# Inner values of a mixture-of-experts layer made by feature, with the weights as the stationary operand

## The reference

```python
w, sel = jax.lax.top_k(probs, K)            # K = 8 of E = 64 experts
w = w / jnp.sum(w, axis=-1, keepdims=True)
...
valid = pos < CAP                            # CAP = 64 rows for each expert
...
h = jax.nn.silu(jnp.einsum('ech,ehi->eci', inp, wg)) * jnp.einsum('ech,ehi->eci', inp, wu)
out = jnp.einsum('eci,eih->ech', h, wd)      # h = 256, i = I = 96
...
g = out_pad[eid, slot] * (w.reshape(-1) * valid.astype(w.dtype))[:, None]
y = jnp.zeros((T, Hd), x.dtype).at[tok].add(g)
```

## Time and profile before

| | us |
|---|---|
| median of 3 runs | 418.92 |
| lowest, highest | 418.79, 421.54 |
| the profiled execution, whole | 416.79 |
| its span, first to last instruction | 415.0 |

### The profile page before, as it was taken

How to read it: one execution, slowest core, us unless ns; L and a number is a source line. 1 busy time by engine, 2 the same in 40 slices (tenths; PEclk the granted TensorE clock), 3 DMA queues, 4 the chain that set the end, 5 groups by cost and what they waited for, 6 DMA issues and landing times.

```text
span 415.0 us, 5198 instructions
## 1 busy us (share of the span) xinstructions
PE 265.8 (64%) x1680; PEld 166.5 (40%) x1680; DVE 230.4 (56%) x519; ACT 130.3 (31%) x230; POOL 163.7 (39%) x165
## 2 busy tenths in 40 slices
PE   4748766599896958877659693620089999960000
PEld 4635535366574626664345432310045555420000
DVE  0747553568777649668462845150057777540393
ACT  5300382007930039511096204010024444230022
POOL 2220022300227742247700287127606478477073
PEclk9897899679997799988969969565579999995555
DMA  7699999970192320962200299200069998966791
GB/s 260 168 133 345 358 386 195 260 206 2 38 134 92 133 86 2 118 111 105 73 2 0 76 343 318 70 25 9 1 194 300 318 192 175 309 99 69 265 383 66
DMA packets 47261, 66.61 MB, mean 161 GB/s; under 512 B 5979, under 2 KB 33241, under 8 KB 47234
## 3 DMA queue, kind: packets, MB, share of 16 engines
q1 hardware_dynamic: 39120, 56.52, 49.3%
q0 software_dynamic: 7680, 9.47, 11.5%
q10 hardware_dynamic: 434, 0.27, 0.2%
HBM read 36.45 MB, written 28.75 MB: 157 GB/s over the span
## 4 chain that ended last, share of the span: by engine, by line
PE 28%; issue 19%; DVE 15%; DMA 12%; ACT 10%; another core or an unknown queue 6%; POOL 5%; SPq 3%; POOLq 0%; DVEq 0%; ACTq 0%
PE M L1052 11%; PE O L1052 6%; DMA acc_d<-xp_t,idx_out 5%; PE SA L1052 3%; DMA early<-early 3%; ACT probs L530 3%; SPq L343 3%; POOL xin_d L451 3%; DVE nmax L763 2%; PE SB L1052 2%; PE O L1398 2%; DVE early L1012 1%; DMA early<-acc_d 1%; ACT xp L553 1%
## 5 line engine op out<-in xcount | busy, mean ns | idle before, releaser
L451 POOL DMA_INDIRECT xin_d<-row,idx_slot x64 | 63.2, 988 | 24.7 <-issue 18.8
L489 POOL DMA_INDIRECT acc_d<-xp_t,idx_out x32 | 49.4, 1544 | 34.5 <-DVE idx_out L988 15.1
L471 POOL TENSOR_TENSOR early<-early 128x1024 f32<-128x1024 f32 x4 | 8.5, 2133 | 86.3 <-ACT early L540 86.3
L1052 PE MATMUL SA<-early 96*128 96x256 bf16 (+1 forms) x128 | 24.4, 325 | 20.1 <-ACT early L594 9.5
L1052 PE MATMUL SB<-early 96*128 96x256 bf16 (+1 forms) x128 | 23.9, 319 | 6.4 <-DVE nmax L763 5.0
L763 DVE TENSOR_REDUCE nmax<-SA 128x4 f32<-128x1024 f32 x16 | 19.5, 1218 | 13.2 <-PE SA L1052 13.2
L1398 PE MATMUL O<-con,probs 128*128 128x128 f32 x40 | 9.2, 319 | 26.2 <-DMA probs<-xin_d 26.2
L1052 PEld LDWEIGHTS SA<-early 96*128 96x128 bf16 (+1 forms) x128 | 12.3, 110 | 31.5 <-issue 12.4
L763 DVE TENSOR_REDUCE nmax<-SB 128x4 f32<-128x1024 f32 x16 | 19.5, 1220 | 9.6 <-PE SB L1052 5.3
L659 ACT ACTIVATE xp<-M 128x96 f32<-128x96 f32 x32 | 8.0, 251 | 51.8 <-PE M L1052 47.8
L1052 PE MATMUL O<-xf,early 128*128 128x256 f32 x64 | 18.6, 445 | 6.4 <-DMA early<-weights 5.2
(11 more groups left out here) (201 smaller groups left out, 644.3 us busy)
## 6 DMA issues: line engine op xcount, KB each, us to landing
gu_sb<-wgu SPq DMA_DIRECT2D x20, 384.0 KB
acc_d<-zeros SPq DMA_DIRECT2D x3, 2176.0 KB, 19.0
early<-early SPq DMA_DIRECT2D x48, 128.0 KB, 5.4
early<-acc_d SPq DMA_DIRECT2D x24, 256.0 KB, 7.5
xin_d<-zeros SPq DMA_DIRECT2D x1, 5136.0 KB, 23.2
early<-wgu SPq DMA_DIRECT2D x12, 384.0 KB
wd_sb<-wd SPq DMA_DIRECT2D x20, 192.0 KB
probs<-xin_d SPq DMA_DIRECT2D x20, 160.5 KB
```

Source lines behind the costliest of these rows:

```text
L451: nc.gpsimd.indirect_dma_start(xin_d, bass.IndirectOffsetOnAxis(ap=idx_slot[:, t, k:k + 1], axis=0), row[:, t, :], None, bounds_check=SLOT ...
L471: nc.gpsimd.tensor_tensor(rest[:], qk[:], parts[:, :, 0], ALU.subtract).then_inc(S["rest_r"], 1)
L489: nc.gpsimd.indirect_dma_start(acc_d[p % CHAINS], bass.IndirectOffsetOnAxis(ap=idx_out[:, p:p + 1], axis=0), yw[:, p % YRING, :], None, bo ...
L1052: return nc.tensor.matmul(o, l, r, start=start, stop=stop)
```

## The change

The gate and up product swaps its operands: the weights are stationary, [128 features x 96], and the gathered rows move, 64 columns. For gate and for up, for each expert and for each half of the features, there is one matmul, eight a pair in place of four. The results stand by feature: `M[0:96]` with gate in columns 0 to 127 and up in 128 to 255, the 128 rows of both experts side by side. So `hid` is made in the form in which the down product takes it. The turn on PE and the copy on ACT go, with their semaphores. The row weight can't be a scalar of each partition any more while features stand on the partitions; it now scales the eviction of the down product, which has rows on the partitions, once for each expert. The factor 0.5 moves into `hid`. PE works on three pairs at once in place of four. The load of rows `p + 10` waits for the evictions of pair `p`, which now read its gathered rows last.

```diff
@@ -379,7 +378,7 @@
             follows = {(p - LATE - RING if p - LATE - RING < RING else p - RING): p for p in range(RING + LATE, PAIRS)}
             for p in range(PAIRS):
                 if p + GRING < PAIRS:
-                    sp.wait_ge(S["hid"], 2 * (p + 1))
+                    sp.wait_ge(S["yw"], 2 * (p + 1))
                     sp.wait_ge(S["idx_out"], p + 1)
                     load_rows(p + GRING)
                 if p in follows:
...
-                pool.wait_ge(S["yw"], p + 1)
+                pool.wait_ge(S["yw"], 2 * (p + 1))
                 if p >= CHAINS:
 
                     pool.wait_ge(S["scat"][p % CHAINS], 16 * (p // CHAINS))
@@ -650,26 +649,24 @@
             pipelined(act, iteration)
 
 
-            for i in range(PAIRS + 3):
+            for i in range(PAIRS + 2):
                 if 1 <= i <= PAIRS:
                     p = i - 1
                     act.wait_ge(S["gu_mm"], p + 1)
                     if p >= 2:
                         act.wait_ge(S["hgate"], p - 1)
-                    nc.scalar.activation(htanh[:, p % 2, :], M[:, p % 2, 0:INNER], ACT.Tanh, scale=0.5).then_inc(S["htanh"], 1)
-                if 2 <= i <= PAIRS + 1:
+                    nc.scalar.activation(htanh[:, p % 2, :], M[0:INNER, p % 2, 0:P], ACT.Tanh, scale=0.5).then_inc(S["htanh"], 1)
+                if i >= 2:
                     p = i - 2
-                    act.wait_ge(S["hid_mm"], p + 1)
-                    if p >= 2:
-                        act.wait_ge(S["wd_mm"], p - 1)
-                    nc.scalar.activation(hid_f[:, p % 2, :], slot[p % 2][0:INNER, 512:512 + P], ACT.Copy).then_inc(S["hid_ev"], 1)
-                if i >= 3:
-                    p = i - 3
                     act.wait_ge(S["wd_mm"], p + 1)
                     if p >= YRING:
                         act.wait_ge(S["scat"][(p - YRING) % CHAINS], 16 * ((p - YRING) // CHAINS + 1))
-
-                    nc.scalar.activation(yw[:, p % YRING, :], slot[p % 2][:, 0:D], ACT.Copy, scale=0.5).then_inc(S["yw"], 1)
+                    for e in range(2):
+
+                        h = slice(e * CAP, (e + 1) * CAP)
+                        c = D + 2 * p + e
+                        nc.scalar.activation(yw[h, p % YRING, :], slot[p % 2][h, 0:D], ACT.Copy, scale=gath(p)[h, c:c + 1]
+                                             ).then_inc(S["yw"], 1)
 
             for t in range(TILES):
                 act.wait_ge(S["fshift"], t + 1)
@@ -994,17 +991,13 @@
                 if i >= 1:
                     p = i - 1
                     dve.wait_ge(S["htanh"], p + 1)
-                    nc.vector.scalar_tensor_tensor(hgate[:, p % 2, :], htanh[:, p % 2, :], 1.0, M[:, p % 2, 0:INNER],
+                    nc.vector.scalar_tensor_tensor(hgate[:, p % 2, :], htanh[:, p % 2, :], 1.0, M[0:INNER, p % 2, 0:P],
                                                    ALU.add, ALU.mult).then_inc(S["hgate"], 1)
                     dve.wait_ge(S["hgate"], p + 1)
                     if p >= 2:
-                        dve.wait_ge(S["hid_mm"], p - 1)
-                    for e in range(2):
-
-                        h = slice(e * CAP, (e + 1) * CAP)
-                        c = D + 2 * p + e
-                        nc.vector.scalar_tensor_tensor(hid[h, p % 2, :], hgate[h, p % 2, :], gath(p)[h, c:c + 1],
-                                                       M[h, p % 2, INNER:2 * INNER], ALU.mult, ALU.mult).then_inc(S["hid"], 1)
+                        dve.wait_ge(S["wd_mm"], p - 1)
+                    nc.vector.scalar_tensor_tensor(hid[:, p % 2, :], hgate[:, p % 2, :], 0.5, M[0:INNER, p % 2, P:2 * P],
+                                                   ALU.mult, ALU.mult).then_inc(S["hid"], 1)
 
 
             def halves_added(t):
...
@@ -1403,27 +1396,21 @@
                     pe.wait_ge(S["xin"], p + 1)
                     pe.wait_ge(*loaded(p))
                     if p >= 2:
-                        pe.wait_ge(S["hid"], 2 * (p - 1))
+                        pe.wait_ge(S["hid"], p - 1)
+                    for u in range(2):
+                        for e in range(2):
+                            for c in range(NC):
+                                m = mm(M[0:INNER, p % 2, u * P + e * CAP:u * P + (e + 1) * CAP], place(p)[0][:, e, c, u, :],
+                                       xin[:, p % 2, c, e * CAP:(e + 1) * CAP], c == 0, c == NC - 1)
+                    m.then_inc(S["gu_mm"], 1)
+                if i >= 2:
+                    p = i - 2
+                    pe.wait_ge(S["hid"], p + 1)
+                    if p >= 2:
+                        pe.wait_ge(S["yw"], 2 * (p - 1))
                     for e in range(2):
                         h = slice(e * CAP, (e + 1) * CAP)
-                        for c in range(NC):
-                            m = mm(M[h, p % 2, 0:2 * INNER], xin[:, p % 2, c, h],
-                                   place(p)[0][:, e, c].rearrange("p u i -> p (u i)"), c == 0, c == NC - 1)
-                    m.then_inc(S["gu_mm"], 1)
-                if 2 <= i <= PAIRS + 1:
-                    p = i - 2
-                    pe.wait_ge(S["hid"], 2 * (p + 1))
-                    if p >= 2:
-                        pe.wait_ge(S["hid_ev"], p - 1)
-                    nc.tensor.transpose(slot[p % 2][0:INNER, 512:512 + P], hid[:, p % 2, :], ident).then_inc(S["hid_mm"], 1)
-                if i >= 3:
-                    p = i - 3
-                    pe.wait_ge(S["hid_ev"], p + 1)
-                    if p >= 2:
-                        pe.wait_ge(S["yw"], p - 1)
-                    for e in range(2):
-                        h = slice(e * CAP, (e + 1) * CAP)
-                        m = mm(slot[p % 2][h, 0:D], hid_f[:, p % 2, h], place(p)[1][:, e])
+                        m = mm(slot[p % 2][h, 0:D], hid[:, p % 2, h], place(p)[1][:, e])
                     m.then_inc(S["wd_mm"], 1)
 
 
```

More of the change, by code:

```diff
@@ L181, in build @@
         flat = xp[:].rearrange("p t h m -> p (t h m)")
-        htanh, hgate, hid = (flat[:, i * 2 * INNER:(i + 1) * 2 * INNER].rearrange("p (g s) -> p g s", g=2)
-                             for i in range(3))
-        gath_b = flat[:, 6 * INNER:6 * INNER + (GRING - in_probs) * ROW].rearrange("p (g r) -> p g r", g=GRING - in_probs)
+        htanh, hgate = (flat[0:INNER, i * 2 * P:(i + 1) * 2 * P].rearrange("p (g s) -> p g s", g=2) for i in range(2))
+        gath_b = flat[:, 4 * P:4 * P + (GRING - in_probs) * ROW].rearrange("p (g r) -> p g r", g=GRING - in_probs)
         def gath(p):
@@ L189, in gath @@
             return gath_a[:, r] if r < in_probs else gath_b[:, r - in_probs]
-        hid_f = mix_a[:].rearrange("p t h d -> p (t h d)")[0:INNER, 0:2 * P].rearrange("p (g s) -> p g s", g=2)
+        hid = mix_a[:].rearrange("p t h d -> p (t h d)")[0:INNER, 0:2 * P].rearrange("p (g s) -> p g s", g=2)
         flat = xp_t[:].rearrange("p t j q -> p (t j q)")
@@ L264, in build @@
                   "idx_out", "gt_mm", "xin", "gu_mm", "htanh",
-                  "hgate", "hid", "hid_mm", "hid_ev", "wd_mm", "yw", "fadd", "fpair", "fstat", "fmv", "fvar", "fshift",
+                  "hgate", "hid", "wd_mm", "yw", "fadd", "fpair", "fstat", "fmv", "fvar", "fshift",
                   "frstd", "fout", "stored", "passed"):
```

## The result

The changed kernel takes 477.12 us (median of 4 runs, 476.67 to 477.41) where the kernel before takes 420.23 in the same set: the ratio is 1.140, 95% interval 1.135 to 1.145. I had predicted 422.2. The profiled execution has a span of 475.6 us, 60.6 over that of before.

What follows compares the result with a forecast made beforehand. Scatters with their landings (2.27 us a step) bound the kernel before; PE at 2.43 would bound the new one. Last scatter 3.3 us later: span 418.3, run 420.1, plus 2.1 to the median: 422.2 us, range 420 to 424.5.

Steps and rivals of the forecast that it cites:

- The start: Start of the experts' stage: clock 1.00 after 306.8 us, first down product at 308.4 where it was 308.69.
- the cycle: PE's time for a pair in the experts' stage: 0.58 + 0.37 + 1.48 = 2.43 us against 2.00.
- Rival D: Experts' stage: clock falls as the array streams less; at 0.50 a pair takes over 4 us, some 60 us; chance 0.04.
- rival B: Gate and up product: records cost moving passes alone, 1.98 us a pair, not slower, 418.5 us; chance 0.13.
- The price of a record: Gate and up product: loading 96 stationary columns sets the pace, 0.084 us a record, bounds 0.054 and 0.111.
- C: Gate and up product: loads cost as for 128 columns, 2.84 us a pair, 435 us in all; chance 0.07.
- PE as the new bound: Experts' stage: PE's 2.43 us a pair exceeds the scatters' 2.27, so PE sets the pace.
- +0.8%: Whole kernel: predicted time of 422.2 us as a change from the median of 418.92.
- The two halves of the eviction: ACT after the down product: two scaled halves take 0.85 us, bounds 0.78 and 0.94, where one took 0.39.
- DVE and the handovers: Between product and down product: DVE instructions near 0.29 us each, four handovers of some 0.05; DVE hidden before and after.
- The moved wait: SP's load of rows p+10 waits for the scaled eviction of p, about one PE cycle later: free.
- rival E: Experts' stage: scatter stalls add to slower PE, two or three of 1 to 2 us, 424 to 427; chance 0.15.

Runs made afterwards that it cites:

- the run in blocks: Changed kernel, but pairs 0 to 7 and 16 to 23 stream 96 gathered rows a matmul, the other pairs 64: 425.16 us, ratio 1.009.
- 96 rows: Changed kernel, but each of the product's eight matmuls streams 96 gathered rows in place of 64, the extra results unread: 403.36 us, ratio 1.007.
- four wide pairs: Changed kernel, but pairs 0 to 3 alone stream 96 gathered rows in each product matmul; pairs 4 to 31 stream 64: 406.50 us, ratio 1.012.
- the matmuls ahead: Changed kernel plus 28 unread matmuls of 128x128 by 512 columns on PE before the experts' stage; all pairs stream 64: 399.95 us, ratio 0.995.
- 128 rows: Changed kernel, but each of the product's eight matmuls streams all 128 gathered rows in place of 64, half unread: 414.19 us beside 400.27.
- the run with the scaled eviction alone: Kernel before, product and turn kept; only row weights move to the eviction in two halves, and row loads wait for it: 405.28 us, ratio 1.014.
- the run that goes wide there: Changed kernel, but pairs 16 to 31 stream 96 gathered rows in each product matmul, pairs 0 to 15 stream 64: 430.23 us beside 402.30.

## Why the prediction was wrong

**The step that failed is "The start".** It took from the earlier trace rows that the clock is 1.00 from 306.8 us on, and carried that over. But in the earlier trace rows the clock rose while the old product ran, which streams 192 columns a matmul; I used the rise as if it belonged to the place in the program and not to what PE does there. In the changed kernel it never comes, and each of the three pieces of the cycle takes 1.7 to 1.9 times as long: 2.51, 1.05 and 0.62, against 1.33, 0.58 and 0.37 with the clock up (the run in blocks). Of the 4.18 - 2.00 = 2.18 us that a pair gained, 1.90 are the clock and 0.28 the new form.

**Rival D had it, with 60 us, and I gave it 0.04.** What I held against it was a row with the clock at 1.00 over eight records of 64 moving columns. That stretch lies behind work that had brought the clock up. It shows that such records keep a full clock, which the experiments bear out (28 narrow pairs at 1.00), and nothing on whether they raise it from half. D was also put as a clock that falls during the stage; measured, it doesn't fall, it fails to rise. The page of the Trainium skill that I cited for rival B (TensorE: Matmul & The Clock Gate) also says, in its Part 1, The HAM clock gate, that PE's clock is low after idle time and rises when PE is kept busy. The trace agrees on the first half and not on the second: 32 pairs with PE busy for every microsecond of the windows, and 0.50 to the end.

**The price of a record was right, the cycle somewhat too long.** I had 0.084; the narrow product at full clock is 1.33/16 = 0.083, and 0.164 at half. But the cycle is 2.28, not 2.43: I added the whole tail of 0.22 to the product, most of which lies in the piece of the chain that follows and was counted there already (0.58 and 0.37 are measured from start to start). The order of the terms was right: it is the load of 96 columns, not the 64 streamed, that sets the pace, so rival B's 1.98 is out, and so is C's 2.84. The section of the Trainium skill that I cited for B (TensorE: Matmul & The Clock Gate, Back-to-back issue gap) gives its rule by moving columns for a single matmul, and says itself that in a stream of loads and matmuls both set the spacing. The trace agrees with the latter: 0.083 where the moving columns alone would give 0.054.

**PE as the new bound: right in kind.** With the clock up, a step of 2.28 is level with the scatters' 2.27, and the time is within 1.2% of the kernel before (1.007 with 96 rows, 1.012 with four wide pairs, 0.995 with the matmuls ahead). With 128 rows PE's 2.70 sets the end. The changed kernel's own instructions on a clock that is up from the start are the run with 28 matmuls ahead, at 0.995 (interval 0.991 to 0.999), so my +0.8% would have been somewhat high there too. A part of that may be the first products at full clock, which the forecast had at half; no run separates it.

**The other terms.** The two halves of the eviction take 0.47 and 0.48 with the handover between, 0.98 together, where I had 0.85 and called the upper bound 0.94. DVE and the handovers were hidden, as said. The moved wait I had called free; the run with the scaled eviction alone says that this part costs 1.4% (0.5 to 2.2) where PE is quick, by a way that isn't separated. The stalls of the scatters (rival E) played no part: at 4.18 a pair POOL waits for ACT at nearly every scatter.

## What to carry to other kernels

Where a stage begins after PE has been idle, its clock is part of what a change can break: look in the rows at which instructions the clock rose, and ask whether the new ones would raise it too. A row at 1.00 shows that work of its kind can keep the clock, not that it can raise it. A change that loads weights more often and streams less should be tried with a few dense matmuls ahead of the stage before its form is given up: here that turned +14% into -0.5%, each beside the kernel before of its own set; the changed kernel itself ran only in the first.

## What the runs showed of the hardware that I had not expected

- A PE that is busy in every window, with loads of 96 columns and 64 streamed, stayed at 1.2 GHz for the whole stage: from 304.6 to 438.8 us in the changed kernel (busy without a break from 306.8 to 433), and 62 us until pair 16 in the run that goes wide there. With 80, 96 or 128 columns streamed between the same loads the clock rose within the first pairs.
- The same narrow work kept 2.4 GHz once it was there: 28 pairs behind four wide ones, and all 32 behind 28 added matmuls. After 8.02 us of idle time it was back at 1.2 GHz and stayed; after 3.30 us of idle time ahead of the stage it fell as well, after 1.09 us (in the kernel before) it didn't.
- In one execution the granted clock stood at 0.65 wherever it is at 1.00 in the others, while 0.50 was as ever. Records of the product, which are 0.085 apart at 1.00, came there at steps of 0.085 and about 0.15 in turn, and the cycle was 2.96 (1.80 + 0.73 + 0.44, rounded, in its chain). What brought that on is open.
- The kernel before has medians of 420 to 422 us in two sets and 400 to 402 in the two others, on other chips. Nothing here explains the difference; all comparisons are inside a set.
